# A three-stage attention block on one core: self-attention in chunks of 512 rows, its second normalisation brought inside it

## The reference

```python
x = x + xattn(ctx, ctx, layernorm(x), ...)            # cross-attention over 1601 context rows
x = x + attn(layernorm(x), W_w, W_b, proj_w, proj_b, ln_g, ln_b, rpb)
x = x + ffn(layernorm(x), w_gate, w_up, w_down)

def attn(x, ...):
    q, k, v = split(x @ W_w.T + W_b)                   # 16 heads of 16 columns
    a = q @ k.T / sqrt(256)                            # per sequence: 64 x 64, causal mask
    w = softmax(a + bias)                              # bias: relative positions, per head
    y = x + (w @ v) @ proj_w.T + proj_b
    return layernorm(y) * ln_g + ln_b
```

## Time and profile before

| | us |
|---|---|
| median of 3 runs (1678.31 to 1681.15) | 1679.34 |
| profiled execution, device time | 1679.94 |
| its span in the trace | 1678.0 |
| cross-attention | 0 to 1248.0 |
| set-up of self-attention | 1248.0 to 1317.0 |
| its 16 steps and their drain | 1317.0 to 1449.7 |
| its tail | 1449.7 to 1468.6 |
| feed-forward up to its integer input | 1468.6 to 1499.7 |
| rest | 1499.7 to 1678.0 |

### The profile page before, as it was taken

How to read it: one execution, slowest core, us unless ns; L and a number is a source line. 1 busy time by engine, 2 the same in 40 slices (tenths; PEclk the granted TensorE clock), 3 DMA queues, 4 the chain that set the end, 5 groups by cost and what they waited for, 6 DMA issues and landing times. The chain is left out here.

```text
span 1678.0 us, 55602 instructions
## 1 busy us (share of the span) xinstructions
PE 1451.8 (87%) x24345; PEld 1019.8 (61%) x24345; DVE 1111.4 (66%) x1735; ACT 893.9 (53%) x1188; POOL 856.2 (51%) x567
## 2 busy tenths in 40 slices
PE   4789999999999999999999999999958388358608
PEld 2356777776777776777776677777644377333206
DVE  7756666666666666666666666666635599685984
ACT  1446665556566555666555566656543144434752
POOL 5567666556666555666655566655305355621000
PEclk9899999999999999999999999999988588768858
DMA  5553354443345444345444334444213300010001
GB/s 169 127 140 101 104 128 117 115 140 101 101 114 129 111 125 125 101 105 128 115 118 138 101 101 113 124 114 111 62 53 75 77 1 0 1 57 0 0 0 51
DMA packets 84295, 154.93 MB, mean 92 GB/s; under 512 B 15376, under 2 KB 47896, under 8 KB 84064
## 3 DMA queue, kind: packets, MB, share of 16 engines
q1 hardware_dynamic: 82704, 150.52, 34.5%
q10 hardware_dynamic: 1360, 0.98, 0.2%
HBM read 61.08 MB, written 2.20 MB: 38 GB/s over the span
## 5 line engine op out<-in xcount | busy, mean ns | idle before, releaser
L638 DVE TENSOR_REDUCE MXP<-W_PS 128x1 f32<-128x512 f32 x768 | 499.1, 687 | 284.8 <-PE W_PS L450 284.8
L534 ACT ACTIVATE PR<-S_PS 128x1024 f32<-128x1024 f32 (+1 forms) x416 | 424.6, 1022 | 260.2 <-PE S_PS L398 252.2
L344 POOL TENSOR_TENSOR K_HI<-K,MCOL 128x512 f16<-128x512 f32 (+1 forms) x224 | 219.0, 978 | 427.2 <-ACT K L542 426.0
L346 POOL TENSOR_TENSOR K_LO<-K,K_HI 128x512 f16<-128x512 f32 (+1 forms) x224 | 291.9, 1303 | 17.6
L450 PE MATMUL W_PS<-STK,QS 105*128 105x512 f16 (+1 forms) x1024 | 269.8, 335 | 9.0 <-POOL STK L371 4.8
L398 PE MATMUL S_PS<-QS,STK 105*128 105x128 f16 (+1 forms) x3328 | 256.1, 220 | 1.0 <-DVE QS L652 1.0
L413 PEld LDWEIGHTS O_PS<-PR,V 128*17 128x17 f32 x13312 | 190.8, 97 | 80.0 <-issue 59.9
L413 PE MATMUL O_PS<-PR,V 128*17 128x64 f32 x13312 | 231.4, 220 | 8.4 <-ACT PR L534 7.4
L433 PE MATMUL W_PS<-WV_HI,CTX_HI 128*128 128x256 f16 (+1 forms) x832 | 228.3, 274 | 1.6 <-DVE WV_LO L611 1.4
L398 PEld LDWEIGHTS S_PS<-QS,STK 105*128 105x128 f16 (+1 forms) x3328 | 201.4, 99 | 44.8 <-DVE QS L652 1.1
L433 PE MATMUL W_PS<-WV_HI,CTX_LO 128*128 128x256 f16 (+1 forms) x832 | 227.8, 274 | 0.0
(11 more groups left out here) (219 smaller groups left out, 1720.6 us busy)
## 6 DMA issues: line engine op xcount, KB each, us to landing
CTX<-in_ctx_t SPq DMA_DIRECT2D x64, 800.5 KB, 5.9
STK<-K_HI SPq DMA_DIRECT2D x256, 128.0 KB, 2.5
STK<-K_HI SPq DMA_DIRECT2D x256, 72.1 KB, 2.1
STK<-K_LO SPq DMA_DIRECT2D x128, 128.0 KB, 2.6
STK<-K_LO SPq DMA_DIRECT2D x128, 72.1 KB, 2.1
QSTK<-STK SPq DMA_DIRECT2D x12, 192.0 KB
SK<-QK_HI SPq DMA_DIRECT2D x8, 256.0 KB, 5.2
SQS<-QK_HI SPq DMA_DIRECT2D x8, 256.0 KB, 5.0
```

Of the source, the lines that this page charges most:

```text
L344: pool.tensor_tensor(K_HI[:, m, lo:hi], k32, zero, ALU.add).then_inc(k_hi, 1)
L346: pool.tensor_tensor(K_LO[:, m, lo:hi], k32, K_HI[:, m, lo:hi], ALU.subtract).then_inc(k_lo, 1)
L534: nc.scalar.activation(PR[0:m, par, :], S_PS[par][0:m, :], ACT.Exp).then_inc(p_sb, 1)
L638: dve.tensor_reduce(MXP[:, j, at:at + 1], bank[:, :], AX.X, ALU.max).then_inc(mx_done, 1)
```

## The change

- **Chunks.** Transposes, QK and V units are made per chunk of four tiles (512 rows). Two chunks are made ahead of the first step, the units of chunks 2 and 3 stand inside steps 0 to 7 (table `BESIDE`).
- **Block-diagonal K.** QZ and its VectorE operations are gone. KZ holds K with zeroed blocks (GpSimd zeroes both buffers once), and SyncE fills it: per chunk 12 transfers of 64 KB into SQS and 24 of 32 KB into KZ. A score product gives 64x64 and there are 32 in a step in place of 16 of 128x64.
- **Step.** T becomes one VectorE instruction, with three T buffers and one S_PS buffer. On VectorE the sums stand at the end of a step, on GpSimd SUB stands ahead of NORM.
- **Tail.** Both last normalisations run in pieces (tiles 0 to 9, 10 to 13, 14 and 15), the first within steps 13 to 16, with a chain of 12 small operations in place of ScalarE's root (`scale_rows`). The feed-forward input is transposed and its maxima are taken here. `proj_b` comes in by a row of ones.
- **Weights.** `w_gate` is rounded and turned in the set-up of self-attention. The feed-forward function handles only `w_up` and `w_down`.

```diff
...
-        for dst, m0, parts in ((SK, 2, (QK_HI, QK_LO, QK_HI)), (SQS, 0, (QK_HI, QK_HI, QK_LO))):
...
-        def queries(s, u):
...
+BESIDE = {
+    0: [("TN", 2, 0), ("TN", 2, 1), ("QK", 2, 0)], 1: [("QK", 2, 1), ("QK", 2, 2)], 2: [("QK", 2, 3), ("VV", 2, 0)], 3: [("VV", 2, 1)],
...
+NORMS = [(0, 10), (10, 14), (14, 16)]
+ADDED = {13: (0, 1, 2), 14: (3, 4, 5), 15: (6, 7, 8), 16: (9,)}
...
+        for r in range(TILES // 4):
+            u = r % 2
+            sp.wait_ge(sm["qk_lo"], 4 * r + 2)
+            if r >= 2:
+                sp.wait_ge(sm["s_ps"], 4 * (r - 1))
+            for c in range(4):
+                for q, part in enumerate((QK_HI, QK_HI, QK_LO)):
+                    sp.dma_start(SQS[32 * q:32 * q + 32, u, c::4, :], part[32 * c:32 * c + 32, u, 0:2, :]).then_inc(stacked[r], 16)
+            sp.wait_ge(sm["qk_lo"], 4 * r + 4)
+            if r < 2:
+                sp.wait_ge(sm["zeroed"], r + 1)
+            for c in range(4):
+                for q, part in enumerate((QK_HI, QK_LO, QK_HI)):
+                    for a in range(2):
+                        lo = 32 * q + DH * a
+                        sp.dma_start(KZ[lo:lo + DH, u, c::4, a, :], part[32 * c + DH * a:32 * c + DH * a + DH, u, 2:4, :])\
+                            .then_inc(stacked[r], 16)
...
+        for x in SETUP:
+            setup(x)
+        for s in range(STEPS):
+            if live(s):
+                r, lo = s // 4, s % 4 * P
+                if s % 4 == 0:
+                    pe.wait_ge(stacked[r], 16 * PARTS)
+                need(pe, sm["t_a"], s)
+                for j in range(PAIRS):
+                    for w in range(2):
+                        cols = slice(lo + w * SQ, lo + (w + 1) * SQ)
+                        for a in range(2):
+                            last = pe.matmul(S_PS[SQ * a:SQ * (a + 1), (2 * j + w) * SQ:(2 * j + w + 1) * SQ], SQS[0:96, r % 2, j, cols],
+                                             KZ[0:96, r % 2, j, a, cols], start=True, stop=True, skip_group_check=True)
+                last.then_inc(sm["s_ps"], 1)
...
+            for x in BESIDE.get(s, []):
+                setup(x)
...
+        pool.wait_ge(sm["wg_max"], 3)
+        pool.tensor_tensor(blk, blk, wide[0], ALU.mult).then_inc(sm["wg_int"], 1)
+        pool.memset(KZ[:, 1].rearrange("p j a c -> p (j a c)").bitcast(F32), 0.0).then_inc(sm["zeroed"], 1)
+        for x in SETUP[:6]:
+            setup(x)
...
+        for s in range(STEPS):
+            if live(s):
+                pool.wait_ge(sm["t_max"], s + 1)
+                pool.tensor_tensor(T[:, s % 3], T[:, s % 3], MX[:, s % 2].unsqueeze(3).broadcast_to([P, PAIRS, 2, SQ]),
+                                   ALU.subtract).then_inc(sm["t_sub"], 1)
+            if live(s - 1):
+                t = s - 1
+                pool.wait_ge(sm["t_sum"], 2 * t + 2)
+                pool.tensor_tensor(T[:, t % 3], T[:, t % 3], SM[:, t % 2].unsqueeze(3).broadcast_to([P, PAIRS, 2, SQ]),
+                                   ALU.mult).then_inc(sm["t_norm"], 1)
...
+        def add_rows(tiles):
+
+            for t in tiles:
+                n = 2 * t
+                dve.scalar_tensor_tensor(XN[:, t, :], XN[:, t, :], MV[:, t, 0:1], LG[:, :], ALU.subtract, ALU.mult).then_inc(sm["x2"], 1)
+                dve.wait_ge(sm["x2"], n + 1)
+                dve.wait_ge(sm["xb"], t // 4 + 1)
+                dve.scalar_tensor_tensor(X[:, t, :], XN[:, t, :], RS[:, t:t + 1], X[:, t, :], ALU.mult, ALU.add).then_inc(sm["x2"], 1)
+                dve.wait_ge(sm["x2"], n + 2)
+                dve.bn_stats(STAT[:, t, :], X[:, t, :]).then_inc(sm["y_stat"], 1)
...
+            if s == 13:
+                dve.wait_ge(sm["y_stat"], 11)
+                scale_rows(*NORMS[0], 0)
+            add_rows(ADDED.get(s, ()))
+            if live(s - 1):
+                t = s - 1
+                dve.wait_ge(sm["t_exp"], t + 1)
+                need(dve, sm["t_norm"], t - 1)
+                dve.tensor_reduce(SM[:, t % 2], T[:, t % 3], AX.X, ALU.add).then_inc(sm["t_sum"], 1)
...
+        for c in range(4):
+            dve.tensor_scalar(XI[:, c], turned(XR, c), INV[:, 0:1], None, ALU.mult).then_inc(sm["xi"], 1)
+            dve.wait_ge(sm["xi"], c + 1)
+            dve.tensor_copy(XR[:, c, 0], XI[:, c]).then_inc(sm["xt_hi"], 1)
+            dve.wait_ge(sm["xt_hi"], c + 1)
+            dve.tensor_tensor(XR[:, c, 1], XI[:, c], XR[:, c, 0], ALU.subtract).then_inc(sm["xt_lo"], 1)
```

More of the change, by code:

```diff
@@ L891, in _ @@
+        for r in range(TILES // 4):
+            sp.wait_ge(stacked[r], 16 * PARTS)
     @block.tensor
     def _(pe):
[L893 to L913, removed]
@@ L1019, in _ @@
-        for i in range(TILES):
-            nc.scalar.activation(XN[:, i, :], XN[:, i, :], ACT.Identity, bias=VT[:, i:i + 1], scale=RS[:, i:i + 1])\
-                .then_inc(sm["y_normal"], 1)
+                nc.scalar.activation(T[:, s % 3], T[:, s % 3], ACT.Exp, scale=1 / 16).then_inc(sm["t_exp"], 1)
+            if s == 16:
+                act.wait_ge(sm["chain"], CHAIN * 2)
+                normal_again(range(0, 4))
+            if s == 17:
+                normal_again(range(4, 10))
+            for x in BESIDE.get(s, []):
+                setup(x)
@@ L1023, in _, with setup @@
+        act.wait_ge(sm["chain"], CHAIN * 4)
+        normal_again(range(10, 14))
+        setup(ENDING[0])
+        setup(ENDING[1])
+        act.wait_ge(sm["chain"], CHAIN * 6)
+        normal_again(range(14, 16))
+        setup(ENDING[2])
     @block.gpsimd
     def _(pool):
+        def setup(x):
+            kind, r, i = x
+            if kind == "QK":
+                n, m = number[x] + 1, qk_rows(i)
+                pool.wait_ge(sm["qk_32"], n)
+                pool.tensor_tensor(QK_LO[:, r % 2, m, :], QK32[:, (n - 1) % 3, :], QK_HI[:, r % 2, m, :], ALU.subtract)\
+                    .then_inc(sm["qk_lo"], 1)
@@ L1163 @@
+        maximum(1)
+        dve.wait_ge(sm["y_stat"], 16 + 14)
+        scale_rows(*NORMS[2], 4)
+        add_rows(range(*NORMS[2]))
+        dve.wait_ge(sm["y_stat"], 16 + 16)
+        scale_rows(*NORMS[2], 5)
+        for i in range(2, len(MAXIMA)):
+            maximum(i)
+        dve.wait_ge(sm["xm"], len(MAXIMA))
+TURN = {8: 0, 16: 1}
 GATE_SCALED = 2
@@ L1244, in groups @@
         return [(k, range(o, min(o + 3, outs))) for o in range(0, outs, 3) for k in range(ins)]
[L1246 to L1254 removed]
+    WT_FIRST = [sum(len(groups(x)) for x in range(w)) for w in range(3)]
     block = ctx.enter_context(nc.Block())
```

656 lines of the change are left out of this document (335 added, 321 removed), and 5 rows, old and new, of tables (BESIDE, SETUP).

## The result

The changed kernel takes 1730.79 us (median of 4 runs, 1729.84 to 1731.75) against 1680.03 (4 runs, 1678.31 to 1681.15): ratio 1.0303, 95% interval 1.0285 to 1.0321. It is 3% slower.

The account below looks back on a forecast made before the run. VectorE's 7.34 us of work was taken to pace each step, the other engines waiting. Terms -21.7 + 80.6 + 15.8 - 21.1 = +53.6 us gave span 1731.6, device time 1733.5, called 1734; range 1693 to 1768.

Parts of the forecast that it names:

- The ring: Plain steps: sums, NORM, transposes, copy, PV, Y, y and back to the sums close a loop of 9.42 us.
- (b): The 15 periods from S(0) to S(15): 191.4 us against 110.8, +80.6.
- Step 13: Chain of 12 small operations, aggregates and three added rows ahead of the sums on VectorE: +7.3 us.
- Steps 0 to 7: Steps that also hold the units of chunks 2 and 3: 10.3 us extra taken, bounds 0 and 20.
- the clock term: TensorE slowed after 4.4 us gaps, on PV, Y and transposes: 1.9 us a step taken over 15 steps.
- (a): Set-up up to the first S: S(0) at 1295.3 against 1317.0, -21.7 us.
- (c): S(15) to the end of self-attention: 56.6 us taken against 40.8, +15.8.
- (d): Feed-forward input after self-attention: 10.0 us against 31.1, -21.1.
- Clock holds: Rival: TensorE stays at full clock in the steps, +20.5 us, 1700; chance .16.
- Clock down throughout: Rival: TensorE at its lower speed in all steps, 13.5 us each, +92.7 us, 1773; chance .11.
- Dear transfers: Rival: small set-up transfers cost 1.08 to 1.2 us each, S(0) 17 to 21 later, 1752 to 1755; chance .07.
- The faster rival: Rival: no loop through late sums forms, steps run at 5.8 us, -50.8 us, 1629; chance .06.

Follow-up runs that it names:

- (1): Changed kernel with VectorE's sums and reciprocal of the tile before put back at the head of the step; one execution, 1678.88 us.
- experiment 3: Changed kernel with 14 unused products of 512 columns behind Y in TensorE's gap in steps 8 to 15; one execution, 1723.33 us.
- experiment 4: Changed kernel with GpSimd making QK_LO of chunk 0 ahead of the w_gate product and the second zeroing; one execution, 1719.52 us.
- experiment 7: Changed kernel with steps reordered on TensorE (transposes one step later), VectorE (sums ahead of y) and ScalarE (exponential ahead of copy); 1657.05 us, ratio .9875.
- experiment 6: Kernel before the change with QZ of all but the first steps cut to one column in 64; one execution, 1675.60 us.

## Why the prediction was right

**The ring** (b) is the whole case, and the experiments show it by moving one thing at a time: the sums alone (1) gave back all of the loss. Plain steps of 9.42 at full clock: 9.6 measured (experiment 3). Clock 1.9 a step: 1.7. Its parts were put together differently: I laid 1.6 on PV and Y; in fact the transposes, first behind the gap, lose .93 in four of the five plain steps and .65 in the other, PV .1 to .8, Y 0 to .8. That 1.9 and 1.7 lie so close is in part luck. Step 13 was given 9.42 + 1.9 + 7.3 = 18.6 and took 18.7; step 14 15.3 and took 16.1. Steps 0 to 7 were given 9.42 x 8 + 10.3 + 15.2 = 100.9 and took 94.6. For clock and units together I had given 25.5 there, 15.2 and 10.3; over eight steps of 9.6 they came to 17.8. No run parts the two in these steps. The rows show that the clock term is not owed in steps 4 and 5, where units fill TensorE's gap (transposes at 1.09 behind gaps of .58 and 1.77), and is in steps 2, 3, 6 and 7 (1.94 to 1.97 behind 4.17 and 4.18). Steps 0 and 4, 12.7 and 12.9, are where the units wait for XLO. The total of (b) is 5.5 below the forecast.

**(a)** was mis-sized by 3.7. Of these 1.9 are SyncE's start (1273.3 for 1271.4): the zeroing ended .5 later, and the first two QK_LO, which let SyncE go, took 1.86 each and not 1.16, 1.4. Another 1.4 is the issue at .64 and not .60. That GpSimd's list, w_gate and zeroing, stood ahead of the transfers was right (experiment 4).

**(c)** and **(d)** hold within .4. Inside (c), S(15) to the last sums took 24.2 (21.2 without clock loss) and VectorE's part behind them 32.0 (30.7). No run takes the tail apart.

**The rivals.** Clock holds: no, .74 over the plain steps; experiment 3, which keeps it up in steps 8 to 12, gives back 8.5 there. Its argument in favour, that Y still takes 1.99 after gaps of 1.33, was misread from the trace of the kernel before. Behind the very gap of the earlier trace rows stand

```profile
1392.75 1.91 PE L951 MATMUL O_PS<-XHI,VS 128*16 128x64 f32 x64
1394.59 2.73 PE L961 MATMUL Y_PS<-WP,XLO 128*128 128x256 f32 x8
```

and the Y at 1.99 in the earlier trace rows belongs to the next step, which has no such gap. Of the six Y behind gaps of 1.18 to 1.36 there, one is at 1.99 and five take 2.48 to 3.78. That speaks against this rival, and for the forecast. Clock down throughout: no, Y is at 1.99 in three of five plain steps. Dear transfers: no, .64. The 1.08 at 256 KB that this rival starts from is not typical of its own trace: the 24 issues of 256 KB took .60 to 1.99, median 1.27. The faster rival, that the ring does not form, is what experiment 7 made by order alone. It was priced at 5.8 a step and 1629, and 6.0 a plain step gave 1657: steps 0 to 7, which it gave no units, took 68.0 in place of 46.4, and S(0) came 4.3 later. So there was a gain in the change (ratio .9923 with both old orders, .9875 with the order of experiment 7), and the order turned it into a loss (1.0303).

**What the prediction missed** is on the side of the kernel before. It said that VectorE's 7.34 paced the steps and the others waited for it. But a ring of the same length closes there. The rows had most of it: T at 1392.66, maxima, SUB to 1397.36, sums at 1398.48. Between them stands the exponential:

```profile
1397.39 1.06 ACT L1013 ACTIVATE T<-T 128x1024 f32<-128x1024 f32 x1 [1.34 <-POOL T L1050]
```

It starts .03 behind SUB and ends .03 ahead of the sums, and T of the next tile follows at 1400.04, 7.38 behind the first. In nine of the sixteen steps the sums start .03 behind the end of the exponential, in five more within .15. So VectorE's list and the ring bound the step together. It did not matter for the forecast, but it is why QZ's removal was worth so little by itself (experiment 6).

## What to carry to other kernels

Ahead of an edit that takes work from the busiest engine, go round every chain that returns to its start within one step, in the order in which each engine's list has it, and add it up; the longest of them, and not the next busiest engine, can set the next pace. Do the same for the kernel as it is: an engine that never pauses may share its pace with such a chain. An instruction that an in-order engine issues behind one which waits for a third engine inherits that wait; the sums, moved from behind y to the head of their step, gave back 52 us here. Put extra work of a step behind what others wait for, not ahead.

## What the runs showed of the hardware

TensorE's granted clock answered to what filled the gap within a step: with 4.36 us of waiting it was .74 over five steps, and with 3.2 us of products in that gap and 1.34 left it was 1.00. The length of the gap alone does not tell it: the kernel before, from 1330 to 1400, had gaps of 1.2 to 1.3 us in four of its steps, TensorE busy in 60.4 of the 70.0 us, and was at .82. What else decides stays open.

Issuing a transfer took SyncE .60 to .64 us at 32, 64 and 72 KB; of the changed kernel's 144 issues three took longer, 1.16 to 1.66. At 256 KB it took .60 to 1.99, median 1.27.

GpSimd's QK_LO took 1.16 us, and 1.86 while VectorE rounded and clipped w_gate beside it. The clip (L1240, 128x1536) took 1.79 us beside QK_LO in the changed kernel and .96 in experiment 4, where GpSimd was idle meanwhile; the rounding (L1238, same shape) took 4.23 beside the zeroing of KZ in both.
